# Three dense node stages of a graph network joined into one chain per tile

## The reference

```
# layer 0: GIN with a batch norm over all nodes
h = relu(h @ W1.T + b1) @ W2.T + b2
h = (h - mean(h, axis=0)) * rsqrt(var(h, axis=0) + eps) * gamma + beta
x = x + h
# layer 1: two GATv2 convolutions with self loops
h0 = relu(layernorm(x))
h  = relu(layer_norm(gatv2_conv(h0, ...1), g1, be1) + h0)
h2 = layer_norm(gatv2_conv(h, ...2), g2, be2)
x  = x + (h2 + h)
```

## Time and profile before

| | us |
|---|---|
| median of 3 runs | 5102.72 |
| lowest and highest | 5097.22, 5115.78 |
| profiled execution, its own time | 5100.17 |
| its span in the profile | 5098.4 |
| mean granted TensorE clock | 0.81 |

### The profile page before, as it was taken

The page is one execution under the profiler, slowest core; times in us unless marked ns, Lnnn a source line. Parts: engine busy times, 40 slices in busy tenths (PEclk is TensorE's granted clock), DMA queues, the critical chain, the costliest instruction groups (busy, mean ns, idle before and its releaser), DMA issues. The chain is left out here.

```text
span 5098.4 us, 66002 instructions
## 1 busy us (share of the span) xinstructions
PE 3325.3 (65%) x14192; PEld 1875.4 (37%) x14192; DVE 3272.3 (64%) x10437; ACT 2689.1 (53%) x7707; POOL 2888.7 (57%) x2835
## 2 busy tenths in 40 slices
PE   2232368544986558888598899958845649943333
PEld 2222323222655523333365334325522225533322
DVE  2212279786997746666687788869957868843333
ACT  1222289796769836566376577736647735520000
POOL 6565677687975466564287555315566500036665
PEclk7666689755999979999799899979977879965555
DMA  7222288797669945554598454459959956732232
GB/s 293 80 76 77 67 269 279 272 406 271 198 189 304 302 139 168 166 167 159 160 330 259 140 161 154 148 176 338 341 182 324 336 160 224 230 128 90 91 85 63
DMA packets 667077, 1019.82 MB, mean 200 GB/s; under 512 B 90963, under 2 KB 275316, under 8 KB 664816
## 3 DMA queue, kind: packets, MB, share of 16 engines
q1 hardware_dynamic: 598864, 877.29, 51.5%
q0 software_dynamic: 65856, 113.13, 8.1%
q10 hardware_dynamic: 2016, 25.69, 1.2%
HBM read 640.44 MB, written 381.14 MB: 200 GB/s over the span
## 5 line engine op out<-in xcount | busy, mean ns | idle before, releaser
L982 DVE TENSOR_TENSOR conv_logits_leaky<-conv_logits_z,conv_logits_sloped 128x512 f32<-128x512 f32 x784 | 507.3, 684 | 182.7 <-issue 102.8
L916 ACT ACTIVATE conv_logits_sloped<-conv_logits_z 128x512 f32<-128x512 f32 x784 | 452.9, 598 | 234.7 <-issue 78.5
L878 PE MATMUL conv_logits_z<-conv_logits_hdT,conv_logits_wsum 128*128 128x512 f32 x784 | 398.3, 652 | 89.3 <-issue 46.7
L1248 PE MATMUL conv_aggregate_part<-conv_aggregate_weighed,conv_wlc 128*128 128x512 f32 x784 | 359.7, 602 | 38.0 <-DVE conv_aggregate_weighed L1330 38.0
L885 PE MATMUL conv_logits_z<-conv_diffT,conv_logits_wl 128*128 128x512 f32 x784 | 358.9, 600 | 27.9 <-DVE conv_logits_leaky L982 25.4
L364 DVE TENSOR_TENSOR_SCAN gine_edges_sumT<-gine_edges_keep,gine_edges_sumT,gine_edges_msgT 128x512 f32<-128x512 f32 x49 | 62.7, 1280 | 439.4 <-ACT gine_edges_msgT L406 355.7
L1982 PE MATMUL mean_edges_counts_ps<-mean_edges_ident,mean_edges_counts 1*128 1x1 f32 x392 | 91.2, 350 | 351.9 <-DVE mean_edges_counts L2006 215.3
L117 POOL DMA_INDIRECT AGG<-gine_edges_rows,idx x196 | 194.0, 990 | 184.2 <-ACT gine_edges_rows L411 102.5
L111 POOL DMA_INDIRECT conv_logits_hdx<-HX,idx x196 | 188.1, 960 | 165.0 <-DMA gine_finish_yT<-YT 95.8
L1497 PE MATMUL conv_nodes_o_ps<-conv_nodes_wmean,conv_nodes_hT 128*128 128x128 f32 x1568 | 225.6, 287 | 81.5 <-ACT conv_nodes_hT L1579 76.9
L878 PEld LDWEIGHTS conv_logits_z<-conv_logits_hdT,conv_logits_wsum 128*128 128x128 f32 x784 | 151.2, 204 | 337.5 <-issue 329.9
(11 more groups left out here) (298 smaller groups left out, 10268.5 us busy)
## 6 DMA issues: line engine op xcount, KB each, us to landing
conv_aggregate_alpha<-ALPHA SPq DMA_DIRECT2D x392, 256.0 KB, 5.1
HX<-gine_finish_hx SPq DMA_DIRECT2D x98, 512.0 KB
AGG<-gine_edges_zero ACTq DMA_DIRECT2D x14, 1792.0 KB
gine_mlp_x<-x SPq DMA_DIRECT2D x98, 256.0 KB
gine_mlp_agg<-AGG SPq DMA_DIRECT2D x98, 256.0 KB
YT<-gine_mlp_yT SPq DMA_DIRECT2D x98, 256.0 KB
gine_finish_x<-x SPq DMA_DIRECT2D x98, 256.0 KB
gine_finish_yT<-YT SPq DMA_DIRECT2D x98, 256.0 KB
```

The lines of the kernel that those rows point to most:

```text
L878: pe.matmul(z[h][:, :], wsum[:, h * D:(h + 1) * D], hdT[j % 3][:, :], start=True, stop=True).then_inc(z_done[0], 1)
L916: act.activation(sloped[(H * (2 * j + c) + h) % S][:, :], z[h][:, :], ACT.Copy, scale=SLOPE).then_inc(sloped_made[c], 1)
L982: dve.tensor_tensor(leaky[H * c + h][:, :], z[h][:, :], sloped[(H * (2 * j + c) + h) % S][:, :], ALU.max).then_inc(leaky_made[c], 1)
L1248: last = pe.matmul(part[n % 2][:, :], g.wlc[:, h * D:(h + 1) * D], weighed[n % 2][:, h, :], start=(h == 0), stop=(h == H - 1))
```

## The change

`gine_finish` and both calls of `conv_nodes` go, and `node_chain` takes their place: one stage over the 98 tiles, in which a tile stays in SBUF from the batch norm to X2. HX, H2 and X2 are still stored, HX and H2 are no longer loaded. The instructions per tile are the old ones but for these: the batch norm moves from ScalarE to VectorE (`tensor_scalar`, SBUF to SBUF); the norm is no longer `apart`; the copy of the turned tile of the first projection moves from VectorE to ScalarE; the bias of the second projection is a TensorE product again instead of a ScalarE copy. VectorE adds residual and both last sums; GpSimd shifts the rows and makes both bases. The weights of both layers are loaded once, in 19 DMAs plus 4 for the last shift, issued after the loads of tile 0. PSUM is shared out as two banks for `rows`, one for each `turned` and two for each `o`.

The 98 gathers from POS that ran beside `conv_nodes` layer 0 move: the 28 for the last 14 edge tiles (EARLY) into `edge_softmax` of layer 0, with one wait and one copy behind them, the other 70, two for each of 35 edge tiles, into `fetch` of `conv_logits` layer 1, each pair 14 tiles ahead of its use and with a small copy per tile. There `keepn` has 3 buffers instead of 4.

```diff
+def node_chain(nc, g):
+        hx = m.sbs("hx", [P, SUB, 2, D], n=HXR)
+        base = [m.sbs(f"base{c}_", [P, SUB, D], n=4) for c in range(2)]
+        norm = Norm(m, "norm", ring=NR)
...
+                sweep(N, [(-3, load), (3, store_hx), (7, store_h2), (11, store_x2)])
...
+                def shift_rows(n):
+                    if n == 0:
+                        wait_alone(pool, beta_in, 16 * SUB, own)
+                    pool.wait_ge(x1_made, n + 1)
+                    past(pool, hx_out[n % HXR], 16 * (n // HXR))
+                    past(pool, base_made[1], n + 1 - HXR)
+                    pool.tensor_tensor(hx[n % HXR][:, :, 1, :], x1[n % NR][:, :, :], beta[:, 1, :, :], ALU.add).then_inc(x1b_made, 1)
+                def base_first(n):
+                    past(pool, sum_made, n - 3)
+                    pool.wait_ge(h1_made, n + 1)
+                    pool.tensor_tensor(base[0][n % 4][:, :, :], hx[n % HXR][:, :, 0, :], beta[:, 0, :, :], ALU.add).then_inc(base_made[0], 1)
+                def base_second(n):
+                    past(pool, x2_made, n - 3)
+                    pool.wait_ge(h2_made, n + 1)
+                    pool.tensor_tensor(base[1][n % 4][:, :, :], h2[n % 4][:, :, :], hx[n % HXR][:, :, 1, :], ALU.add).then_inc(base_made[1], 1)
+                sweep(N, [(3, base_first), (7, base_second), (2, shift_rows), (0, place)])
...
+                sweep(N, [(4, project(0)), (8, project(1)), (3, turn(0)), (7, turn(1)), (0, turn_rows)])
...
+                def batch_norm(n):
+                    dve.wait_ge(y_in[n % YR], 16 * (n // YR + 1))
+                    past(dve, rows_done, n - 1)
+                    dve.tensor_scalar(bT[n % 2][:, :], yT[n % YR][:, :], g.bn_scale[:, :], g.bn_shift[:, :], ALU.mult, ALU.add).then_inc(bT_made, 1)
+                def take_rows(n):
+                    dve.tensor_tensor(x1[n % NR][:, :, :], rows[n % 2][:, :, :], x[n % XR][:, :, :], ALU.add).then_inc(x1_made, 1)
+                    dve.wait_ge(x1_made, n + 1)
+                    norm.take_stats(dve, x1[n % NR], n % NR)
+                    norm.moments(dve, n % NR, n + 1)
+                def sum_second(n):
+                    dve.wait_ge(base_made[1], n + 1)
+                    dve.wait_ge(scaled_made[1], n + 1)
+                    dve.tensor_tensor(flat(scaled[1][n % OUT]), flat(scaled[1][n % OUT]), flat(base[1][n % 4]), ALU.add).then_inc(x2_made, 1)
+                sweep(N, [(2, lambda n: norm.scales(dve, n % NR, n + 1)), (0, batch_norm), (5, scale(0)), (1, take_rows), (9, scale(1)), (5, sum_first), (10, sum_second)])
...
+                sweep(N, [(2, normalize), (4, square(0)), (6, relu), (3, copy_turned(0)), (8, square(1)), (7, copy_turned(1)),
+                          (1, lambda n: norm.root(act, n % NR, n + 1, eps))])
...
@@ conv_logits, layer 1: fetch(j)
+                    if spread:
+                        if j >= EARLY:
+                            wait_alone(pool, place_kept, j + 1 - EARLY, own)
+                        if j + EARLY < N:
+                            look_up(j + EARLY)
...
@@ edge_softmax, layer 0
+                    first = g.NTE - EARLY
+                    for e in range(EARLY):
+                        for s in range(SUB // 2):
+                            gather(pool, pos[:, e, s, :], g.POS[:, :], g.idx[:, 2 + s, first + e:first + e + 1]).then_inc(g.looked, 16)
+                    wait_alone(pool, g.looked, 16 * 2 * EARLY, own)
...
@@ convolutions
-        for layer in range(2):
-            conv_nodes(nc, g, layer, layer == 1)
+        node_chain(nc, g)
```

More of the change, by code:

```diff
@@ L620, in store, with load @@
[L620 to L628 removed]
+                def load(n):
+                    past(sp, x1_made, n + 1 - XR)
+                    sp.dma_start(x[n % XR][:, :, :], node_rows(g.x, n)).then_inc(x_in[n % XR], 16)
+                    past(sp, bT_made, n + 1 - YR)
+                    sp.dma_start(yT[n % YR][:, :], g.YT[n:n + 1, :, :].rearrange("t p j -> (t p) j")).then_inc(y_in[n % YR], 16)
+                    if n == 0:
+                        load_weights()
@@ L632, in _, with place @@
                 make_identity(pool, ident, ident_made, cleared)
[L633 to L639, removed]
                 pool.iota(edge_row[:, :, :, :], pattern=[[TILE, g.NTE], [1, 2], [0, 16]], base=g.NP + 2, channel_multiplier=SUB).then_inc(edge_made, 1)
-                for n in range(g.NTN):
-                    add_beta(n % NB, n // NB)
+                def place(n):
                     if n == 0:
@@ L660, in turn, with step @@
                     last.then_inc(rows_done, 1)
-                pipeline(pe, nb, NB, [(0, turn)])
+                def turn(c):
+                    def step(n):
+                        pe.wait_ge(h2_made if c else h1_made, n + 1)
+                        past(pe, hT_made[c], n)
+                        for a in range(SUB):
+                            last = pe.transpose(turned[c][:, a * P:(a + 1) * P], h2[n % 4][:, a, :] if c else hx[n % HXR][:, a, 0, :], ident[:, :])
+                        last.then_inc(turned_done[c], 1)
+                    return step
@@ L675, in take_stats @@
[L675 to L681, removed]
-                    (3, lambda k, i: norm.scales(dve, k % RING, i * NB + k + 1)),
-                    (0, take_stats)])
+                dve.memset(ones[:, :], 1.0).then_inc(set_once, 1)
@@ L695, in normalize @@
[L695 to L704 removed]
+                act.wait_ge(set_once, 3)
@@ new lines, in square, with step @@
+                def square(c):
+                    def step(n):
+                        act.wait_ge(o_done[c], n + 1)
+                        past(act, std_made[c], n - 1)
+                        for a in range(SUB):
+                            last = act.activation(squares[:, a, :], o[c][n % 2][:, a, :], ACT.Square, accum_out=power[c][n % 2][:, a:a + 1])
+                        last.then_inc(squared[c], 1)
+                        act.wait_ge(squared[c], n + 1)
+                        past(act, rstd_made[c], n - 1)
+                        act.activation(std[c][n % 2][:, :], power[c][n % 2][:, :], ACT.Sqrt, bias=eps[:, :], scale=1.0 / D).then_inc(std_made[c], 1)
+                    return step
```

441 lines of the change are left out of this document (181 added, 260 removed).

## The result

The changed kernel takes 5193.62 us (median of 4 runs, 5186.0 to 5204.4), the kernel before 5103.88 us beside it (4 runs). The ratio is 1.0175 (95% interval 1.0148 to 1.0202): it is slower by 1.75%, where I had forecast 1% faster, and it lies outside the range of 4965 to 5145.

The account below looks back on a forecast made before the run. VectorE was taken to bound the fused stage: 625 us of floor + 101 of port waits + 42 of heads and tails = 768 against 824. With +6 for moved gathers, 5100 - 56 + 6 = 5050 us, range 4965 to 5145.

Parts of the forecast that it names:

- The floors: In the fused stage, per tile: VectorE 6.38 us as the bound, ScalarE 6.19, TensorE 5.69, GpSimd 5.2, DMA 4.1.
- ScalarE's ring: In the fused stage: normalize waits for VectorE's scales, which wait for ScalarE's last root; 6.6 us per step, hidden if VectorE slows.
- Heads and tails: Start and end of the fused stage: first weight loads, TensorE's low clock, last tile's drain, last store; 42 us, between 30 and 60.
- I take it that the shift gets through, GpSimd waits during it and goes next: At each step's start in the chain: only the batch norm waits for GpSimd's addition, 1.16 us per step, 101 us.
- Rival B: Chain: GpSimd gets the port ahead of both shift and batch norm, 2.4 us per step, total 5158; chance 0.15.
- the forecast: Whole kernel: port waits of 0.7 to 1.5 us per step, total 5050 us, own range 5005 to 5090; chance 0.48.
- The sizes of one meeting: Chain: VectorE's batch norm waits for GpSimd's addition and ends at 1.91 instead of 0.75 us, 1.16 us per step.
- the batch norm's meeting: Chain: the batch norm waiting for GpSimd's `base_second` at the port, giving a period of 7.5 us.
- At the upper level after the first steps: Sign in the new stage: TensorE's granted clock would be at its upper level after the first steps.
- Rival D: Chain: TensorE's clock stays at 1.2 GHz, 11.4 us per tile, total about 5440; chance 0.02.
- The moved gathers: `edge_softmax` layer 0: +6 us, between 0 and +12; `conv_logits` layer 1: 0, at most +5.
- GpSimd idles 204/49 = 4.2 us per tile: `conv_logits` layer 1: this idle time hides two gathers, a copy and two waits, 3.5 us, for 35 tiles; cost 0.

Follow-up runs that it names:

- experiment 5: Experiment 2's kernel with the bias products of both layers left out on TensorE, output lacking the biases: ratio 0.9774 to the kernel before, chain 681.6 us.
- experiment 1: Changed kernel with GpSimd's scatter into POS placed ahead of `shift_rows`, nothing else: ratio 0.9996 to the kernel before, chain 803.1 us.
- experiment 2: Changed kernel with GpSimd waiting for the batch norm at the head of each step: ratio 0.9862 to the kernel before, chain 717.8 us.
- experiment 7: Changed kernel plus experiment 2's wait, `conv_logits` look-ups from fetch 7 with lead two, EARLY 9 instead of 14: 5014.9 us, ratio 0.9794 to before.
- experiment 3: Changed kernel with a fifth buffer for `base_second`'s result, so GpSimd waits for a last sum one tile further back: ratio 1.0029 to the kernel before.

## Why the prediction was wrong, step by step

**The floors held.** VectorE 6.38 us and ScalarE's ring 6.6 were forecast; without meetings the step is 6.47. Heads and tails were 42; in experiment 5, where neither port nor clock disturbs, they are 681.6 - 98 x 6.47 = 48. That the port decides, where the two engines meet, and through which wait, was right too.

**The step that failed** is "I take it that the shift gets through, GpSimd waits during it and goes next". I had read GpSimd's release as 0.20 us behind the end of the sum, which put its start 0.08 behind the shift's. It is 0.08 (1408.38 to 1408.46), so GpSimd is 0.05 ahead. Rival B named this very condition, "if GpSimd came 0.1 us earlier than rows 7 say". Then both instructions are caught, not one: 2.2 us per step instead of 1.16. Per tile I had (625 + 101)/98 = 7.41 us; the step is 8.555; 98 x 1.145 = 112 of the 115 us by which the chain missed its 768. Why the release is faster here isn't tested. By the code, GpSimd's additions in `conv_nodes` stood behind `wait_alone`, a wait and an own semaphore instruction, which `base_second` doesn't have.

Rows 7 gave one release of another instruction, and the forecast hung on 0.1 us of it. I called it a tie, and still gave B 0.15 and the forecast 0.48. A tie that recurs in every step is one toss of a coin that counts 87 times: its two sides should have had nearly the same chance, and the range should have reached beyond B.

**The sizes of one meeting** were right: 1.16 forecast for the batch norm, and experiment 1, which leaves only the shift's meeting, has 7.52 us where the forecast had 7.5 (it was for the batch norm's meeting, which costs about the same). B's chain, 625 + 209 + 42 = 876, is 7 short of 883.

**TensorE's clock.** "At the upper level after the first steps" was wrong: 0.69 over the stage. Rival D, always low, was wrong as well. The alternation costs 4.7 us of steps in the kernel after and 36 us in experiment 2. The earlier trace rows had shown 0.95 in `conv_nodes` layer 1 with TensorE busy 163 of 260 us, and I took that as a promise for a stage with another pattern.

**The moved gathers.** edge_softmax: +6 forecast, +9.0 measured, GpSimd last as said; a gather took 1.51 us, not 1.43. conv_logits layer 1: 0 to +5 forecast, +23.0 measured. The step that failed is "GpSimd idles 204/49 = 4.2 us per tile". That idle time is a mean over the running loop and did cover the look-ups there. But the lead of 14 tiles also put look-ups into the burst that fills the ring at the start of the stage, where GpSimd has no idle time and everything waits for it. `keepn`'s shorter ring: 0, as said; experiment 7 has it and takes 542.3 us.

**The sum.** 5050 + 115 + 3 + 23 = 5191; the 5.5 us of the other stages make it 5196.5, and the profiled execution's own time is 5196.56. Rivals A and C: A's period came only once GpSimd was gated; C's, near 8, had another mechanism than the one at work.

## What to carry to other kernels

Where two engines share a port, write down for each instruction that needs it what releases it. If one engine's release is the end of the other's instruction, and that other has port users next, they meet in every round. Then put an engine's port users together and release the other behind the last of them (experiment 2: 165 us for one wait), rather than loosen its wait (experiment 3).

A gap of some tenths of a microsecond, read from another instruction's release, doesn't decide an order. And idle time that is to hide moved work must be read where the work will stand: in the loop, in the filling at its start, and in the stage's end apart.

## What of the hardware I had not expected

- A VectorE instruction of four elements per partition takes 1.25 us instead of 0.16 when it comes 0.05 us behind a GpSimd addition. Its size is no protection.
- GpSimd's scatter does not hold VectorE's `tensor_scalar`: started 0.59 us into a scatter it took 0.55 us (experiment 3), and 0.53 where it started 0.22 us ahead of one (experiment 1). The scatter itself took 1.26 and 1.18 us there, for 0.98 in the kernel after.
- The recorded start of a VectorE instruction isn't its turn at the port. The batch norm is recorded from 1409.68, `shift_rows` from 1409.69, and GpSimd goes first: VectorE's shift ends only at 1409.76.
- TensorE's granted clock changed level many times in one stage (1.16 and 2.08 us for the same eight matmuls, 10 us apart), although TensorE was busy 800 of 884 us in the records. The means of the earlier trace rows, 0.50, 0.94 and 0.95, hadn't prepared me for that.
- A burst of gathers issued by GpSimd (48, 1.25 us apart) goes, from 28 us behind its start, with a ScalarE that does one instruction in 4 to 20 us, its inputs being ready. Fewer gathers in the burst end it sooner. By what path the one holds the other up is open; no run here separates it.
